# The product wq times s in plain f32 in place of three rounded passes, with s copied once

## What is computed

```
for i in range(12):
    qkv = x @ Wqkv[i].T + bqkv[i];  q, k, v = split(qkv, 3)      # 16 heads of 8
    att = einsum('bhqd,bhkd->bhqk', q, k) / sqrt(8)
    y = einsum('bhqk,bhkd->bhqd', att, v)
    x = y @ Wproj[i].T + bproj[i] + x
x = layernorm(x0 + x)
gate, up = x @ (w_gate / 127).T, x @ (w_up / 127).T
out = layernorm(x + (silu(gate) * up) @ (w_down / 127).T)
```

## Time and profile before

| | us |
|---|---|
| median of 3 runs | 369.2 |
| the profiled execution | 370.07 |
| its span, first to last instruction | 368.3 |
| TensorE busy in it | 326.5 |
| VectorE busy | 250.9 |
| ScalarE busy | 200.8 |
| GpSimd busy | 113.8 |

### The profile page before, as it was taken

One profiled execution on the slowest core, in us unless ns is written; L12 is line 12 of the kernel. 1 busy time (PEld: TensorE's weight loads), 2 busy tenths in 40 slices (PEclk: granted clock), 3 DMA queues, 4 the chain that ended last, 5 costly groups with the idle time before them and its releaser, 6 DMA issues.

```text
span 368.3 us, 9534 instructions
## 1 busy us (share of the span) xinstructions
PE 326.5 (89%) x3877; PEld 285.2 (77%) x3877; DVE 250.9 (68%) x688; ACT 200.8 (55%) x457; POOL 113.8 (31%) x103
## 2 busy tenths in 40 slices
PE   8397977979979799797997979979799799999994
PEld 7385956959769597695976959769597698888883
DVE  1048887758577485774857748577585766999975
ACT  2053754847648476484764847648476225454340
POOL 2021452305123051230512305123054220656433
PEclk9789999999999999999999999999999999999999
DMA  8900100101001010010100101001000000010112
GB/s 243 400 6 2 59 0 4 55 2 57 2 2 58 2 56 2 2 57 3 58 2 2 57 2 56 2 2 58 2 2 2 2 2 2 28 28 28 46 44 57
DMA packets 10664, 13.72 MB, mean 37 GB/s; under 512 B 512, under 2 KB 8832, under 8 KB 10496
## 3 DMA queue, kind: packets, MB, share of 16 engines
q1 hardware_dynamic: 8224, 11.35, 9.6%
q10 hardware_dynamic: 2400, 1.80, 1.6%
HBM read 11.04 MB, written 2.10 MB: 36 GB/s over the span
## 4 chain that ended last, share of the span: by engine, by line
PE 74%; DVE 11%; DMA 4%; issue 4%; ACT 4%; POOL 1%; ACTq 0%; POOLq 0%; DVEq 0%
PE ps L858 11%; PE ps L963 11%; PE ps L813 10%; PE ps L815 9%; PE ps L814 9%; PE ps L917 6%; DMA xt<-x_tok 4%; PE ps L874 3%; PE ps L869 3%; PE ps L1042 3%; DVE s_lo L646 2%; ACT s_hi L462 2%; DVE mt L630 2%; PE ps L1031 2%; DVE xt L748 2%
## 5 line engine op out<-in xcount | busy, mean ns | idle before, releaser
L376 POOL TENSOR_TENSOR step_lo<-step,step_hi 128x512 fp32r<-128x512 f32 x44 | 55.1, 1284 | 113.7 <-ACT step_hi L468 113.6
L462 ACT CAST s_hi<-ps 128x512 fp32r<-128x512 f32 x48 | 24.7, 599 | 53.5 <-PE ps L917 53.5
L813 PE MATMUL ps<-state_hi,step_hi 128*128 128x258 f32 x176 | 50.7, 288 | 0.0
L815 PE MATMUL ps<-state_hi,step_lo 128*128 128x258 f32 x176 | 49.9, 283 | 0.0
L814 PE MATMUL ps<-state_lo,step_hi 128*128 128x258 f32 x176 | 49.6, 282 | 0.0
L646 DVE TENSOR_TENSOR s_lo<-ps,s_hi 128x512 fp32r<-128x512 f32 x48 | 29.8, 684 | 27.2 <-ACT s_hi L462 27.2
L858 PE MATMUL ps<-w,gram 128*128 128x128 f32 x352 | 44.0, 278 | 0.0
L963 PE MATMUL ps<-step,gram 128*128 128x128 f32 x352 | 43.6, 277 | 0.3 <-DVE gram L636 0.3
L963 PEld LDWEIGHTS ps<-step,gram 128*128 128x128 f32 x352 | 41.9, 192 | 1.4 <-DVE gram L636 0.4
L858 PEld LDWEIGHTS ps<-w,gram 128*128 128x128 f32 x352 | 41.1, 192 | 1.0
L357 POOL TENSOR_TENSOR wq_lo<-w,wq_hi 128x512 fp32r<-128x512 f32 x12 | 15.2, 1267 | 78.6 <-ACT wq_hi L451 78.6
(11 more groups left out here) (127 smaller groups left out, 626.0 us busy)
## 6 DMA issues: line engine op xcount, KB each, us to landing
w<-weights SPq DMA_DIRECT2D x12, 496.5 KB, 3.6
xchan<-x_chan SPq DMA_DIRECT2D x1, 2048.0 KB, 13.8
out<-xchan SPq DMA_DIRECT2D x7, 256.0 KB, 2.3
xt<-x_tok ACTq DMA_DIRECT2D x4, 256.0 KB, 10.7
xt<-x_tok SPq DMA_DIRECT2D x4, 256.0 KB, 5.2
fw_int<-ffn_weights ACTq DMA_DIRECT2D x1, 576.0 KB, 16.4
out<-xchan SPq DMA_DIRECT2D x2, 128.0 KB, 1.9
cst<-consts ACTq DMA_DIRECT2D x1, 154.5 KB, 4.6
```

Of the source, the lines that this page charges most:

```text
L376: nc.gpsimd.tensor_tensor(group(step_lo, g), group(step, g), group(step_hi_f, g), ALU.subtract).then_inc(step_lo_ready, 1)
L462: nc.scalar.copy(group(s_hi, g), products(S_BANKS[g])).then_inc(s_hi_ready, 1)
L813: nc.tensor.matmul(dst, l_hi, r_hi, start=True, stop=False)
L815: return nc.tensor.matmul(dst, l_lo, r_hi, start=False, stop=True)
```

## The change

wq and s are no longer split; the product is one f32 matmul a group, straight from the weights' slot. s is copied out of PSUM once: groups 0 and 2 by ScalarE, 1 and 3 by VectorE. SyncE's third condition is now the layer's last wq product.

```diff
-        s_hi = sb("s_hi", [P, BATCHES, P], F32R)
-        s_lo = sb("s_lo", [P, BATCHES, P], F32R)
+        s_rows = sb("s_rows", [P, BATCHES, P])
...
-        wq_hi = sb("wq_hi", [P, QUADS, P], F32R)
-        wq_lo = sb("wq_lo", [P, QUADS, P], F32R)
...
                 sp.wait_ge(shift_ready, k + 1)
-                sp.wait_ge(wq_split, k + 1)
+                sp.wait_ge(n_done, GROUPS * (k + 1))
                 sp.dma_start(w[:, k % 2, :], weights[k + 2]).then_inc(w_in[k % 2], 16)
...
-                pool.wait_ge(wq_hi_set, at(1, 1))
-                nc.gpsimd.tensor_tensor(wq_lo[:, :, :].rearrange("p r c -> p (r c)"), w[:, s, WQ:WQ + QUADS * P],
-                                        wq_hi[:, :, :].rearrange("p r c -> p (r c)").bitcast(F32),
-                                        ALU.subtract).then_inc(wq_split, 1)
...
-                act.wait_ge(w_in[s], at(8, 16 - 8 * s))
-                nc.scalar.copy(wq_hi[:, :, :].rearrange("p r c -> p (r c)"), w[:, s, WQ:WQ + QUADS * P]).then_inc(wq_hi_set, 1)
...
                 act.wait_ge(s_done, at(1, 1))
-                for g in range(GROUPS):
-                    nc.scalar.copy(group(s_hi, g), products(S_BANKS[g])).then_inc(s_hi_ready, 1)
+                for g in range(0, GROUPS, 2):
+                    nc.scalar.copy(group(s_rows, g), products(S_BANKS[g])).then_inc(s_even_ready, 1)
...
-                def low_of_s(g):
-                    dve.wait_ge(s_hi_ready, at(GROUPS, g + 1))
-                    nc.vector.tensor_tensor(group(s_lo, g), products(S_BANKS[g]), group(s_hi_f, g),
-                                            ALU.subtract).then_inc(s_lo_ready, 1)
+                def take_s(g):
+                    dve.wait_ge(s_done, at(1, 1))
+                    nc.vector.tensor_copy(group(s_rows, g), products(S_BANKS[g])).then_inc(s_odd_ready, 1)
...
-                for g in range(GROUPS):
-                    low_of_s(g)
+                take_s(1)
+                take_s(3)
...
-                pe.wait_ge(wq_split, at(1, 1))
                 for g in range(GROUPS):
...
-                    pe.wait_ge(s_lo_ready, at(GROUPS, g + 1))
-                    three_pass(ps[:, STEP_BANKS[g], :], wq_hi[:, g, :], wq_lo[:, g, :], group(s_hi, g), group(s_lo, g))\
-                        .then_inc(n_done, 1)
+                    pe.wait_ge(s_odd_ready if g % 2 else s_even_ready, at(2, g // 2 + 1))
+                    nc.tensor.matmul(ps[:, STEP_BANKS[g], :], w[:, s, WQ + P * g:WQ + P * (g + 1)], group(s_rows, g),
+                                     start=True, stop=True).then_inc(n_done, 1)
```

More of the change, by code:

```diff
@@ L117, in build @@
         step_hi_f = step_hi[:].bitcast(F32)
-        s_hi = sb("s_hi", [P, BATCHES, P], F32R)
-        s_lo = sb("s_lo", [P, BATCHES, P], F32R)
-        s_hi_f = s_hi[:].bitcast(F32)
+        s_rows = sb("s_rows", [P, BATCHES, P])
         gk = sb("gk", [P, BATCHES, P])
@@ L228, in build @@
         shift_ready = sem("shift_ready")
-        wq_hi_set = sem("wq_hi_set")
-        wq_split = sem("wq_split")
         s_done = sem("s_done")
-        s_hi_ready = sem("s_hi_ready")
-        s_lo_ready = sem("s_lo_ready")
+        s_even_ready = sem("s_even_ready")
+        s_odd_ready = sem("s_odd_ready")
         n_done = sem("n_done")
```

## The result

The changed kernel takes 372.49 us (median of 13 runs, 369.79 to 374.24) against 369.71 of the kernel before beside it (13 runs, 368.02 to 371.95): ratio 1.007, 95% interval 1.0038 to 1.0101. It is slower by 0.7%, where 368.2 and no measurable change were forecast; the range ended at 370.2, and a loss of over 0.5% had been given a chance of 0.07. The profiled execution took 373.84 us, its span 372.0, against 370.07 and 368.3.

What follows compares the result with a forecast made beforehand. TensorE, 74% of the chain, was taken to bound the kernel. Twelve layers at 0.00, layer 1 at -0.11 and -0.48, layer 2 at -0.46 gave -1.05, say -1.0: 368.2 us from 369.2, 8-in-10 range 366.5 to 370.2.

Steps and rivals of the forecast that it cites:

- 12 x 0.00 - 0.11 - 0.48 - 0.46 = -1.05: Whole kernel: wq product in twelve layers 0.00 each, layer 1 -0.11 and -0.48, layer 2 -0.46 us.
- What else moves in an inner layer: Inner layers: copies, steps and waits of the other engines move, but none delays TensorE; all costed at nothing.
- rival A: Twelve wq products: 512-column record is dear; at 0.465 net +1.65, 370.8 us; chance 0.18.
- rival B: Twelve wq products: record is cheap, 0.42, so 1.6 us more is won, 366.5 us; chance 0.20.
- C: Layers 1 and 2: gains don't come because another VectorE or GpSimd instruction is just behind; 369.2 us; chance 0.10.
- The head: Inner layer, from L917's end to the first wq product: 0.75 us instead of 1.48.
- The product: Inner layer, wq product as eight f32 records of 0.437 plus 0.10 for first weights: 3.60 us against 2.88.
- 0.00 a layer: Inner layer: product starts 0.72 us earlier and lasts 0.72 longer, so L963 starts where it does now.
- vdiag: VectorE, 0.29 us in all layers without wq_lo beside it; in layer 1's chain 0.40 becomes 0.29, -0.11.
- the wait of the third group: Layer 1: L963's third group no longer waits for VectorE's corrected gram; -0.48 us.
- fw: Layer 2, VectorE: 0.56 us alone instead of 1.58 beside wq_lo; L917 then starts 0.60 behind L874, -0.46.
- VectorE's copies: Inner layer: two copies replace four subtractions, each between 0.28 and 0.68 us, upper taken; TensorE waits for none.

Runs made afterwards that it cites:

- the split put back: ScalarE's rounding and GpSimd's subtraction of wq restored as work nobody reads, in the changed kernel with exchanged arms: 366.86 us, ratio 0.9917.
- exchanged arms: Changed kernel with the branch's two arms swapped so the running one stands right behind it: 366.02 us; kernel before with the same swap: 370.12 us.
- the two other kernels with the gap: Waits already satisfied added to TensorE's program: 28 instructions in the kernel before, 374.37 us; 62 in the changed kernel, 371.19 us.

## Why the prediction was wrong

The step that failed is the sum, "12 x 0.00 - 0.11 - 0.48 - 0.46 = -1.05": it has no term for anything outside the layers. "What else moves in an inner layer" asks what the edit does to the other engines' work, and costs that at nothing; that TensorE's program gets 107 instructions shorter, and that this moves all code behind them, was neither in the sum nor in a rival. The rivals A to C all concern the layers. The missing term is +5.2 us: 2.9 at the branch and 2.3 by the clock behind it.

The rule was there to be read: the Trainium skill, "Runtime: NRT & Kernel Launch", section "Instruction fetch mechanics", says that an engine's instructions come in blocks of 256, prefetched in order only, and that a taken branch to outside the two blocks held stops the engine for a fetch. The traces agree as far as they go, with 3.4 to 3.5 us a stop. The profile of before had the signs of it, a gap of 0.62 "issue" at the branch and a queue of instruction fetches in its DMA table, and I did not ask what the edit would do to them.

Point by point in the layers:

- The head, forecast at 0.75, is 0.66 from L904's end in eleven layers: the step from ScalarE to TensorE takes 0.04 there, where I took VectorE's 0.14. In layer 1 it is 0.14.
- The product, forecast at 3.60 with a record of 0.437: the spacing is 0.43, 8 x 0.43 + 0.10 = 3.54. At 0.429 it lies just under the forecast's own 0.432 to 0.444, half way from 0.437 to rival B's 0.42; rival A (dear) is wrong, B (cheap) half right.
- So 0.00 a layer was -0.16 in eleven and -0.06 in layer 1: -1.8 in all. Two small errors of one sign, twelve times, were more than everything I had worked out for layers 1 and 2.
- Layer 1: vdiag at 292 ns, and the wait of the third group gone. Right.
- Layer 2: fw 0.56 as forecast, S 0.61 behind the end of L861 (0.60 forecast). Right, and with the split put back 0.56 is lost again.
- vdiag is 291 to 294 ns in all layers. Right. VectorE's copies take 686 ns, against the 0.68 taken.
- Sum: -1.05 - 1.8 = -2.9. Measured in the layers: -2.95 with exchanged arms (-2.9 and -3.0 in the pairs with the same arms), -2.6 as first run. Most of the difference between the two is in the first group of layer 1: L845 x12 took 1.62 there and 1.34 with exchanged arms, since the lower clock of the token stage reached into it.

The +1.1 at the start is no effect of the change that I could show: 0.4 of it is the tokens, which landed at 17.04 and not at 16.61, and 0.7 the passes behind them (L819 x24 took 5.53, L832 x24 4.84), more of which ran at the lower clock. Layer 1 starts anywhere between 18.95 and 22.61 in the profiles here, of kernels with the same token stage save for fillers. Single executions of the changed kernel lie from 369.79 to 374.24, and those at 373.56 and above all have a mean clock of 0.976, the others 0.981 to 0.989. Behind the gap the clock stays low for 6.8 us in the profile above and for 3.4 in the two other kernels with the gap. The mean clock of an execution doesn't say whether it was low there or at the start, so how the other executions of the changed kernel divide is not shown, nor what decides the length. The block boundaries themselves were not read anywhere, only inferred from shifts, fetch times and counts.

## What to carry to other kernels

Before an edit that changes the number of instructions on an engine, look for what depends on their position: a taken branch behind the edit, and dense runs of short instructions. Put the arm that runs right behind the branch; it cost nothing measurable and took the lottery out (0.25 to 0.41 us at the branch in the six kernels that have it so, 366.02 us for the version that beats both). And when a total comes out wrong, cut the span at two or three landmarks first: here the part under change had gained, and the loss was in one that nobody had touched.

## What the runs showed that I had not expected

- A taken branch over some 431 instructions costs 0.6 to 0.7 us or 3.4 to 3.5, by position alone; where the arm that runs stands right behind the branch, 0.25 to 0.41.
- Idling of 3.4 to 3.5 us, begun at full clock, came with 3.4 to 6.8 us at the lower clock level, which cost up to 2.3 more; the stop of 1.86 us in layer 7, with a wait of 0.68 soon after it, was followed by 3.4.
- A run of 256 short instructions in 1.9 us stopped for 1.86 us in one of the twelve kernels here.
- Fillers are not free: 62 wait instructions whose semaphore had fired kept TensorE from its next product for 4.7 us, some 0.08 us each; 79 kept it for 6.5.
- A plain f32 product with 512 columns is two records, spaced 0.43 us, so 0.86; three rounded passes of it take 0.70. It pays in a layer because the split of s leaves the chain: the head is 0.66 in place of 1.48.
